# A ring of weight tiles moved behind all other buffers, and one stretch of a four-layer decoder in another written-out order

## The reference, cut to what matters

```
x = x + tanh(g_xattn[2]) * L2_xattn(layernorm(x), ctx, ctx, pos, mask, Wq, Wk, Wv, Wo)   # 32 heads of 128, 8 key heads, rotary
x = x + tanh(g_ffn[2])   * L2_ffn(layernorm(x), W_base, b_base, W_router, lora_A, lora_B) # top-2 of 8 low-rank experts on a base product
x = x + tanh(g_xattn[3]) * L3_xattn(layernorm(x), ctx, ctx, Wq, Wk, Wv, Wd)               # 32 heads of 128, rotary, causal
x = x + tanh(g_ffn[3])   * L3_ffn(layernorm(x), ...)
```

## Time and profile before

| | us |
|---|---|
| three runs | 1779.73, 1778.82, 1779.58 (median 1779.58) |
| the profiled execution, its own time | 1779.62 |
| its span in the trace | 1777.8 |
| PE busy | 1747.3 (98% of the span) |
| DVE, POOL, ACT busy | 1208.9, 972.0, 864.3 |
| mean granted TensorE clock | 0.993 |

### The profile page before, as it was taken

The page is one execution under the profiler, slowest core; times in us unless marked ns, Lnnn a source line. Parts: engine busy times, 40 slices in busy tenths (PEclk is TensorE's granted clock), DMA queues, the critical chain, the costliest instruction groups (busy, mean ns, idle before and its releaser), DMA issues.

```text
span 1777.8 us, 27517 instructions
## 1 busy us (share of the span) xinstructions
PE 1747.3 (98%) x8776; PEld 1435.8 (81%) x8776; DVE 1208.9 (68%) x2202; ACT 864.3 (49%) x2459; POOL 972.0 (55%) x808
## 2 busy tenths in 40 slices
PE   7999999999999999999999999999999999999999
PEld 6888887777878888888888888788888888888887
DVE  7566566878876666666666675766666666666685
ACT  7666665725444444434544452345444444444451
POOL 3223232556675665746657463676665656657561
PEclk9999999999999999999999998999999999999999
DMA  6101010121110111101111011111110111101101
GB/s 210 31 13 36 13 34 7 32 92 42 31 48 13 53 35 29 41 18 53 29 35 41 24 41 31 30 54 30 35 41 18 53 29 35 41 18 47 33 16 48
DMA packets 37429, 69.47 MB, mean 39 GB/s; under 512 B 4426, under 2 KB 5194, under 8 KB 37234
## 3 DMA queue, kind: packets, MB, share of 16 engines
q1 hardware_dynamic: 37362, 68.61, 13.0%
HBM read 66.50 MB, written 2.10 MB: 39 GB/s over the span
## 4 chain that ended last, share of the span: by engine, by line
PE 92%; DVE 3%; issue 2%; POOL 1%; ACT 1%; DMA 0%; SPq 0%; POOLq 0%; DVEq 0%; ACTq 0%
PE ps L443 27%; PE ps L445 27%; PE ps L444 27%; PE ps L715 4%; PE ps L696 3%; PE ps L622 1%; PE ps L653 1%; DVE negmax L1598 1%; POOL probs L3442 0%; DVE ot_lo L1631 0%; POOL rope_a L3424 0%; DVE pt_loL L1620 0%; DVE ot_lo L1626 0%; DMA ct_raw<-in_ctx_t 0%; PE ps L1080 0%
## 5 line engine op out<-in xcount | busy, mean ns | idle before, releaser
L3442 POOL TENSOR_TENSOR probs<-probs,rsums 128x512 f32<-128x512 f32 (+1 forms) x160 | 194.7, 1217 | 280.6 <-DVE rsums L1616 280.4
L3424 POOL TENSOR_TENSOR rope_a<-rope_a,rope_b 128x512 f32<-128x512 f32 x160 | 206.6, 1291 | 154.4 <-DVE rope_b L1591 154.2
L443 PE MATMUL ps<-wo_hiL,ot_hi 128*128 128x512 f32 x608 | 249.0, 410 | 3.0 <-DVE ot_lo L1631 2.2
L443 PE MATMUL ps<-xt_hi,wq_hiL 128*128 128x512 f32 x608 | 242.6, 399 | 0.3 <-DVE xt_lo L1526 0.2
L445 PE MATMUL ps<-wo_hiL,ot_lo 128*128 128x512 f32 x608 | 241.5, 397 | 0.0
L444 PE MATMUL ps<-wo_loL,ot_hi 128*128 128x512 f32 x608 | 241.2, 397 | 0.0
L445 PE MATMUL ps<-xt_hi,wq_loL 128*128 128x512 f32 x608 | 237.9, 391 | 0.0
L444 PE MATMUL ps<-xt_lo,wq_hiL 128*128 128x512 f32 x608 | 237.0, 390 | 0.0
L2643 ACT ACTIVATE probs<-ps,negmax 128x128 f32<-128x128 f32 x512 | 182.1, 373 | 88.2 <-DVE negmax L1598 88.1
L2660 ACT CAST ot_hi<-ps 128x512 fp32r<-128x512 f32 (+1 forms) x160 | 90.7, 567 | 256.6 <-PE ps L445 256.2
L3436 POOL TENSOR_TENSOR q_loL<-rope_a,q_hiL 128x512 fp32r<-128x512 f32 x128 | 164.7, 1297 | 28.1 <-ACT q_hiL L2630 28.1
(11 more groups left out here) (232 smaller groups left out, 4239.5 us busy)
## 6 DMA issues: line engine op xcount, KB each, us to landing
raw<-in_L_proj SPq DMA_DIRECT2D x108, 256.0 KB, 2.6
raw<-in_L_out SPq DMA_DIRECT2D x76, 256.0 KB, 2.6
raw<-in_F_w SPq DMA_DIRECT2D x16, 256.0 KB, 2.7
ct_raw<-in_ctx_t SPq DMA_DIRECT2D x8, 256.0 KB, 6.3
x<-in_x SPq DMA_DIRECT2D x8, 256.0 KB, 6.2
cn_raw<-in_ctx SPq DMA_DIRECT2D x8, 256.0 KB, 7.4
out<-x SPq DMA_DIRECT2D x8, 256.0 KB, 2.0
raw<-in_L_kv SPq DMA_DIRECT2D x6, 256.0 KB, 3.0
```

The source lines that it names most:

```text
L443: pe.matmul(dst, l_hi, r_hi, start=start, stop=False)
L3424: gp.tensor_tensor(rope_a[:, a], rope_a[:, a], rope_b[:], ALU.add).then_inc(L.s_rsum, 1)
L3442: gp.tensor_tensor(pv, pv, rsums[:, b % 2].unsqueeze(2).to_broadcast([P, GH, L.keys]), ALU.mult).then_inc(L.s_p, 1)
```

## The change

Two things are changed, and no instruction is added or removed.

**Memory.** `raw` is allocated behind all other tiles, and `st` moves from behind `nbias` to between `probs` and `ot_hi`.

**Order.** The four `middle` lists are permuted. On PE: `keys_queries(1)` comes ahead of `scores(0)`, `transposes(0)` goes behind `scores(2)`, the norm transposes of F2 come earlier, `gates(4)` to `(7)` come in one row behind `experts(2)`. On ACT: `base_weight(1)` to `(3)` go behind `pt_head(7)`, `expert_weight(2)`, `a3.weights(0)` and `a3.weights(1)` go behind `o_head(7)`. On DVE: F2's `norm_rows`, `norm_tail` and `next_stats` are mixed in earlier, `pt_tail(7)` comes ahead of `norm_tail("F2", 2)`. On POOL: the tails of `base_weight` and `add_bias(2)`, `(3)` are placed anew.

```
-        raw = new("raw", [P, RAW, RAW_COLS], F32)
         probs = new("probs", [P, GH * 2 * P], F32)
+        st = new("st", [P, GH * P], F32)
         ot_hi = new("ot_hi", [P, GH * P], F32R)
...
-        st = new("st", [P, GH * P], F32)
         sums = new("sums", [P, 2, GH], F32)
...
         bthr = new("bthr", [P, 1], F32)
+        raw = new("raw", [P, RAW, RAW_COLS], F32)
```

More of the change, by code:

```diff
@@ L1107, in middle @@
                 a2.scores(1, last)
+                a2.fillers(0, last, only=1)
+                a2.keys_queries(3, last)
+                a2.scores(2, last)
                 a2.transposes(0, last)
[L1109 to L1112, removed]
                 a2.fillers(1, last, only=0)
                 a2.fillers(1, last, only=1)
+                a2.heads_out(0, last)
                 a2.transposes(1, last)
@@ L1177, in middle @@
                 products(2, 4)
+                norm_transpose("A3", 0)
                 turn(2, 1)
@@ L2026, in middle @@
                 a2.row_sum(0, last)
-                scale_bias(2)
[L2028 to L2035, removed]
+                a2.evacuate(0, 0, last)
+                a2.row_max(1, last)
+                a2.masked(2, last)
+                a2.row_sum(1, last)
+                a2.masked(3, last)
+                a2.pt_tail(0, last)
+                a2.row_max(2, last)
+                scale_bias(2)
                 a2.evacuate(1, 0, last)
                 a2.evacuate(1, 1, last)
+                a2.ot_tail(0, last)
+                a2.pt_tail(1, last)
                 a2.row_sum(2, last)
-                a2.pt_tail(1, last)
                 a2.evacuate(2, 0, last)
@@ L2043, in middle @@
                 a2.row_max(3, last)
+                a2.next_stats(0, last)
                 a2.pt_tail(2, last)
-                a2.next_stats(0, last)
                 a2.row_sum(3, last)
@@ L2051, in middle @@
                 a2.row_max(4, last)
+                a2.next_stats(1, last)
                 a2.pt_tail(3, last)
-                a2.next_stats(1, last)
+                a2.masked(5, last)
+                norm_rows("F2", 1)
                 a2.row_sum(4, last)
-                a2.masked(5, last)
                 a2.residual(2, last)
                 a2.ot_tail(3, last)
+                a2.masked(6, last)
                 a2.row_max(5, last)
@@ L2061, in middle @@
                 a2.row_sum(5, last)
-                a2.masked(6, last)
                 a2.residual(3, last)
+                norm_tail("F2", 0)
                 a2.ot_tail(4, last)
                 a2.row_max(6, last)
-                norm_rows("F2", 1)
+                a2.masked(7, last)
+                norm_rows("F2", 2)
                 a2.pt_tail(5, last)
+                a2.row_sum(6, last)
                 a2.next_stats(3, last)
-                a2.row_sum(6, last)
-                a2.masked(7, last)
                 a2.residual(4, last)
@@ L2073, in middle @@
                 a2.row_max(7, last)
+                norm_rows("F2", 3)
                 a2.pt_tail(6, last)
-                norm_rows("F2", 2)
                 a2.row_sum(7, last)
-                norm_tail("F2", 0)
+                norm_tail("F2", 1)
                 a2.residual(5, last)
+                a2.next_stats(4, last)
                 a2.ot_tail(6, last)
-                norm_rows("F2", 3)
-                norm_tail("F2", 1)
-                a2.next_stats(4, last)
+                a2.next_stats(5, last)
+                a2.pt_tail(7, last)
                 norm_tail("F2", 2)
-                a2.pt_tail(7, last)
                 norm_rows("F2", 4)
@@ L3077, in middle @@
                 norm_head("A3", 3)
+                norm_rows("A3", 4)
+                a3.weights(5)
+                a3.begin(3, 0)
                 a3.begin(5, 0)
-                norm_rows("A3", 4)
+                a3.begin(3, 1)
                 norm_rows("A3", 5)
-                a3.begin(3, 1)
                 norm_head("A3", 4)
```

185 lines of the change are left out of this document (90 added, 95 removed).

## The result

The changed kernel takes **1758.89 us**, the median of four runs (1757.82 to 1759.71). The kernel before, on the same chip, took 1779.20 (four runs). The ratio is 0.9889, with a 95% interval of 0.9877 to 0.9902, so the change saves 20 us. The profiled execution took 1759.71 us, its span is 1757.9.

The account below looks back on a forecast made before the run. PE, busy 1747.3 of 1777.8 us, was taken as the bound. From 1779.6 us, 9.5 for the order (3.8 + 0.4 + 5.3) and 9.1 for the addresses were subtracted, giving 1761.0 us; range 1757 to 1772.

Parts of the forecast that it names:

- Order, 9.5 us: In `middle`, the new lists remove PE waits of 3.8 and 0.4 us plus 5.3 us at the lower clock; bounds 8.0 to 10.5.
- 2.5 us of slack forecast: At `heads_out(7)`, PE asks for pt_lo 5.9 us after `transposes(7)` starts; DVE has it ready after 3.4 us at the latest.
- two-part account: In `middle`, `a3.weights(1)` behind `taken(3)` on ACT and `pt_tail(7)` ahead of `norm_tail(2)` on DVE together remove the 3.8 us wait.
- What it takes back, 0 to 1 us: New PE waits from the reordered `middle` lists: sum 0, with a bound of 1 us for what the layout misses.
- The steps feared most: In `middle`: `turn(2, 0)`, tightest with 0.4 us of slack, and `base_weight(3)`, done near 1076.0 with 6.8 us of slack.
- Clock, 5.3 us: From 1080.26 to 1091.43 us PE took 11.2 us for work of 5.9 us at the upper level; 5.3 us go with the wait.
- Addresses, 9.1 us: Output projections: `ot` at a multiple of 64 bytes saves 5 ns on each of 1824 matmuls; bounds 0 to 10.9 us.
- what sets `ot` apart from every other stationary operand is its address: Output projections: `ot` lies 32 bytes off a multiple of 64, other PE operands at multiples; excess taken as 5 ns a matmul.
- The transposes, nothing: Transposes of `probs` and `xn` might gain from the new addresses, 0.01 us a step at most; nothing was counted.
- Addresses do nothing: Rival: something else about `out_proj` makes `ot` slow and stays, so only the order gains; 1770.1 us, chance 0.29.
- The wait moves: Rival: PE stops some 4 us elsewhere in F2 and the clock falls, price 9.1 us; 1770 or 1779, chance 0.08.
- `ot` reads worse because it begins at the same offset as `wo`: Rival: in output projections, stationary `ot` and moving `wo` hinder each other, 1.8 us per nanosecond; 1781 or 1792, chance 0.03.

Follow-up runs that it names:

- e1: The changed kernel's new order with the old addresses (`raw` ahead of `probs`, `st` behind `nbias`); 1768.33 us, ratio 0.9942.
- e12: The kernel before with one ACT line moved: `a3.weights(1)` behind `taken(3)` instead of behind `pt_head(7)`; 1768.13 us, ratio 0.9949.
- e2: The kernel before with its old order, but tiles placed as in the changed kernel; 1769.21 us, ratio 0.9948.
- e4: The changed kernel with `probs`, `st`, `vt`, `xn`, bias and constants 32 bytes off, `ot` at another multiple of 64; 1769.15 us, ratio 0.9952.
- e5: The changed kernel with `ot_hi` and `ot_lo` alone 64 bytes further up, tiles behind them by 128; 1769.97 us, ratio 0.9953.
- e9: The changed kernel with the first tile at byte 512 instead of 384, so every tile moves by 128 bytes; 1760.56 us, ratio 0.9895.
- e7: The changed kernel with `ot` ahead of `probs` at the same remainder by 512, the tiles behind 32 bytes off; 1756.85 us, ratio 0.9877.

## Why the prediction was right

The forecast was 1761.0 us with a range of 1757 to 1772; the time is 1758.89, in the range and 2.1 below the forecast.

- **Order, 9.5 us.** e1 puts it at 1777.78 - 1768.33 = 9.4 us. Its pieces are there as named: no wait for pt_lo, clock 1.00, 2.5 us of slack forecast and 5.8 - 3.0 = 2.8 found. The cause (one ACT entry waiting for a DMA, with the casts behind it) is shown by e12, which gets the gain from that entry alone. The prediction's two-part account was broader than it had to be: without `pt_tail(7)` moved on DVE nothing is lost.
- **What it takes back, 0 to 1 us.** No new wait of PE appeared: the three that are left between 1000 and 1160 us are all in the kernel before. The steps feared most (`turn(2, 0)` with 0.4 us of slack, the base weights) don't show.
- **Clock, 5.3 us.** e2 keeps the wait and also the windows at 0.50 and 0.52; the changed kernel and e12 lose both. The two go together, as the sum had it, and the clock is the larger half: e12 gains 1777.37 - 1768.13 = 9.2 us, of which the wait was 3.8.
- **Addresses, 9.1 us.** e2 puts them at 1777.78 - 1769.21 = 8.6 us, e1 against the changed kernel at 1768.33 - 1758.89 = 9.4 by the medians and 1765.5 - 1757.9 = 7.6 by the spans. The 5 ns a matmul were 4.3 by the pitch (0.2329 - 0.2286), so 1824 of them give 7.8 us. Part of the rest lies in the steps behind an `ot` step, which gain as well, as shown above. The size was nearly right.
- **The reason for it was wrong in its number and its nature.** The step that failed is "what sets `ot` apart from every other stationary operand is its address", read as a multiple of 64. e4 and e5 stand at a multiple of 64 and are slow; e9 shifts all and is not. What set `ot` apart was its distance to the operand that streams with it: 32 by 256 where the pairs it was compared with have 0. (One 512-column pair stands at 128 in both kernels: L0's `pt,v` for the second source, as a row of its `v` is 384 bytes. Its steps are too short to price it.) The forecast came out because the tiles moved down by 11040 - 2048 = 8992 = 35 x 256 + 32 bytes, which takes that 32 away. A ring of 11072 bytes (173 x 64) ahead of `ot` would have passed for aligned by my rule; by the table it puts the pair at 64 and costs some 8.6 us (an estimate, 1824 x 4.7 ns).
- **One piece of evidence held and could have led to the distance.** The prediction said that base products show no excess, and none of the traces has one: their steps of twelve (`wt,xt`) have a pitch of 0.2287 in the kernel before, 0.2291 in the changed one and 0.2284 to 0.2294 in all the others. Their rows of 1700 us to the end, before and then after:

```profile
L443 PE MATMUL ps<-wt_hi,xt_hi 128*128 128x512 f32 x32 | 12.7, 398 | 0.0
L444 PE MATMUL ps<-wt_lo,xt_hi 128*128 128x512 f32 x32 | 12.5, 390 | 0.0
```

```profile
L443 PE MATMUL ps<-wt_hi,xt_hi 128*128 128x512 f32 x32 | 12.7, 397 | 0.0
L444 PE MATMUL ps<-wt_lo,xt_hi 128*128 128x512 f32 x32 | 12.5, 390 | 0.0
```

- **A third partner says the same.** The experts' products (`lb,ot`, three matmuls, 24 steps) have `ot` as the stationary operand and do follow its place. The time from their second to their third start is 0.2296 to 0.2305 us on the mean where the distance is 0, and 0.2317 to 0.2330 where it is 32, 64, 128 or 192. They are few, but they bear out the distance with another moving operand, `lb`.
- **The transposes, nothing.** e7 has `probs`, `st`, `xn` and the constants 32 bytes off and is no slower than the changed kernel. Right.
- **Rivals.** *Addresses do nothing* (1770.1): fell, and with it the rule of the Trainium skill (TensorE: Matmul & The Clock Gate, section "Wait — 56ns, not 53.3ns?") as a full account: the rule has no term for an address and gives about 216 ns; measured are 226.7 in undisturbed steps at distance 0 (228.6 on the mean) and 233.3 on the mean at 64. *The wait moves*: no such wait is in the trace. *`ot` reads worse because it begins at the same offset as `wo`*: the exact opposite is the case. The same offset is the fast one; that rival's doubt, which operand stands where against which, was the right question.

e7 (1756.85) is the fastest median, but its interval, 0.9862 to 0.9892, overlaps the changed kernel's, 0.9877 to 0.9902. I do not claim it to be better.

## What to carry to other kernels

On an in-order queue, an entry that waits for a DMA holds back everything behind it; find the entry with the long idle time ahead of it and move that one past what does not need it. Here one line was worth 9 us, over half of it because the idle engine's clock had fallen. And when two groups of matmuls with the same shape differ by a per cent with no idle time, print the addresses of both operands: make them equal by 256 bytes, for each pair, and re-check whenever a tile of an odd size is put ahead of either. That rule is shown here for fp32r with a 128x128 stationary operand, 512 columns and a new stationary operand for every matmul, and for nothing else.

## What the hardware showed that I had not expected

- The start-to-start time of a 128x128 by 512-column fp32r matmul depends on the distance of its two SBUF operands by 256 bytes: on the mean 228.6 ns at 0, 232.8 at 32, 233.3 at 64, 232.5 at 128, 229.8 at 192.
- It does not depend on the address itself: all tiles 128 bytes further up, 228.7 ns.
- A shift of the stationary operand `wq` by 64 bytes slowed its products to 233.4 ns in the same way.
- Part of the 228.6 is carried over from what ran just before. Undisturbed steps at distance 0 run at 226.7 ns; behind 128-column transposes, or behind a step at another distance, the intervals are long at first and then fall to 227.
- At the lower clock the distance costs nothing that these traces show: in the windows at 0.50, `wo,ot` matmuls start every 427 ns at distance 32 (before, 1088.02 to 1091.43) and at distance 0 (e2, 1081.06 to 1084.47).
